# Keys and values laid out for their consumer: by strided matmul outputs and two sets of buffers, or by split VectorE writes and one set

## The reference, cut to what matters

```
xn = rms(x, g1)
Q = einsum('bsf,ef->bse', xn, Wq); K = einsum(..., Wk); V = einsum(..., Wv)   # 16 heads of 16
pQ = elu(Q); pK = elu(K)
Q1, Q2 = split(pQ, 2); K1, K2 = split(pK, 2)
kv1 = einsum('bshe,bshd->bsed', K1, V) * SCALE     # per token, over the heads
w1  = einsum('bshe,bsed->bshd', Q1, kv1)
attn = w1 - lmb * w2
```

## Time and profile before

| what | value |
|---|---|
| median of 3 runs | 1002.11 us |
| profiled execution | 997.24 us, its span 995.6 us |
| PE busy | 846.5 us (85%) |
| DVE busy | 644.6 us (65%) |
| ACT busy | 457.9 us (46%) |
| POOL busy | 258.8 us (26%) |
| DMA issues of K and V stores | 32 of 256 KB, median 3.5 us to landing |
| mean granted TensorE clock | 0.927 of full speed |

### The profile page before, as it was taken

The page is one execution under the profiler, slowest core; times in us unless marked ns, Lnnn a source line. Parts: engine busy times, 40 slices in busy tenths (PEclk is TensorE's granted clock), DMA queues, the critical chain, the costliest instruction groups (busy, mean ns, idle before and its releaser), DMA issues. The chain is left out here.

```text
span 995.6 us, 23453 instructions
## 1 busy us (share of the span) xinstructions
PE 846.5 (85%) x8964; PEld 700.0 (70%) x8964; DVE 644.6 (65%) x1464; ACT 457.9 (46%) x943; POOL 258.8 (26%) x323
## 2 busy tenths in 40 slices
PE   6999999998599999957999889988789649999940
PEld 5877778786377777735777778875567539999940
DVE  2577778777347777764555336678797876656438
ACT  2443443443477777735964324553533304444410
POOL 1146653122101123220000000022242043565323
PEclk9999999999699999987999989999989759999985
DMA  8400000000000000001476344452122213465437
GB/s 308 155 17 21 16 21 16 20 7 2 1 2 1 1 2 1 1 1 47 125 194 185 95 111 117 115 187 67 49 85 85 85 32 104 127 179 153 112 96 255
DMA packets 76428, 79.55 MB, mean 80 GB/s; under 512 B 22592, under 2 KB 66496, under 8 KB 75968
## 3 DMA queue, kind: packets, MB, share of 16 engines
q1 hardware_dynamic: 71376, 72.36, 23.5%
q0 software_dynamic: 3968, 5.25, 3.3%
q10 hardware_dynamic: 1008, 0.91, 0.3%
HBM read 50.71 MB, written 27.79 MB: 79 GB/s over the span
## 5 line engine op out<-in xcount | busy, mean ns | idle before, releaser
L712 DVE TENSOR_TENSOR r_prob<-r_pS,const 128x512 f32<-128x512 f32 x128 | 79.4, 682 | 32.4 <-PE r_pS L535 32.4
L1052 DVE SCALAR_TENSOR_TENSOR f_gl<-f_g,small_first,f_gh 128x512 fp32r<-128x512 f32 x64 | 47.3, 747 | 41.1 <-ACT f_gh L990 38.8
L931 PE MATMUL f_pY<-wpjT,f_gh 128*128 128x256 f32 x256 | 65.1, 289 | 0.0
L932 PE MATMUL f_pY<-wpjT,f_gl 128*128 128x256 f32 x256 | 62.7, 279 | 0.0
L931 PEld LDWEIGHTS f_pY<-wpjT,f_gh 128*128 128x128 f32 x256 | 48.1, 188 | 15.3 <-issue 13.4
L2223 POOL DMA_INDIRECT sum_dram<-e_yo,y_id x24 | 39.5, 1647 | 69.6 <-ACT e_yo L2312 61.8
L984 ACT ACTIVATE f_g<-f_pH 128x512 f32<-128x512 f32 x64 | 38.0, 594 | 39.2 <-PE f_pH L920 38.4
L838 POOL TENSOR_SCALAR t_ey<-t_es 128x8 f32<-128x8 f32 x4 | 1.0, 256 | 211.4 <-ACT t_sqrow L1770 211.4
L920 PE MATMUL f_pH<-f_xh,wfcT 128*128 128x512 f32 x128 | 53.2, 415 | 1.4 <-DVE f_xl L1046 1.4
L2342 DVE SCALAR_TENSOR_TENSOR e_hl<-e_pH,e_hh 128x320 fp32r<-128x320 f32 x64 | 27.7, 484 | 38.5 <-ACT e_hh L2305 38.4
L920 PE MATMUL f_pH<-f_xl,wfcT 128*128 128x512 f32 x128 | 51.8, 405 | 0.0
(11 more groups left out here) (292 smaller groups left out, 2447.8 us busy)
## 6 DMA issues: line engine op xcount, KB each, us to landing
kv_dram<-att_res SPq DMA_DIRECT2D x32, 256.0 KB, 3.5
t_ring<-kv_dram SPq DMA_DIRECT2D x128, 64.0 KB, 2.3
wi<-L_ffn_wi SPq DMA_DIRECT2D x8, 1024.0 KB, 5.7
wo<-L_ffn_wo SPq DMA_DIRECT2D x8, 1024.0 KB, 8.7
x_res<-L_attn_x SPq DMA_DIRECT2D x8, 512.0 KB, 5.0
q_dram<-att_res SPq DMA_DIRECT2D x8, 512.0 KB, 3.1
t_q<-q_dram SPq DMA_DIRECT2D x64, 64.0 KB, 2.8
x_dram<-x_res SPq DMA_DIRECT2D x8, 512.0 KB, 3.0
```

Of the source, the lines that this page charges most:

```text
L712: dve.tensor_tensor(prob[t % 2][:, r, :, :], pS[r][:, :, :], dec[:, r, :, :], ALU.mult)\
L931: pe.matmul(out, gh[c % 4][:, cols], net.wpjT[:, c, :], start=(c == 0 and t % 2 == 0), stop=False, skip_group_check=True)
L932: mm = pe.matmul(out, gl[c % 4][:, cols], net.wpjT[:, c, :], start=False, stop=(c == NH - 1), skip_group_check=True)
L1052: dve.scalar_tensor_tensor(out=gl[c % 4][:, :], in0=g[c][:, :], scalar=net.lnw[:, c:c + 1], in1=gh[c % 4][:, :], op0=ALU.mult, op1=ALU.sub ...
```

## The change

The special matmuls go. All six items become plain items: two matmuls of 128 columns by 512 tokens. The layout is made when the results are written to SBUF instead. For each K or V item, VectorE issues two instructions of 64 partitions by 512 elements: rows 0 to 63 and rows 64 to 127 of the item, both to partitions 0 to 63 of `res`, each to every fourth word (a step of 16 bytes). K and V are then stored by one transfer of 512 KB each, from 64 partitions, with 8 KB in one run for each.

There is one set of `res` in place of two. VectorE waits, at the head of each part, for the store of this part in the batch just before. The last V item of the last batch is written by ScalarE, behind a wait for the store of the batch before, and SyncE waits for a semaphore of its own for it. The counts in the waits of the fourth phase are changed to suit.

```diff
-    res = [[spare[:, (3 * p + n) * KD * SEQ:...] for n in range(3)] for p in two]
+    part = lambda n: spare[:, n * RUN * SEQ:(n + 1) * RUN * SEQ].rearrange("p (t i) -> p t i", i=RUN)
+    res = [part(n) for n in range(3)]
+    res_q = res[0].rearrange("p t i -> p (t i)")[:, 0:KD * SEQ].rearrange("p (k t) -> p k t", k=KD)
...
 # SyncE
-                sp.wait_ge(item_ready.sem, item_ready.after(ITEMS * b + KD * (n + 1)))
+                last = b == BATCH - 1 and n == 2
+                sp.wait_ge(item_ready.sem, item_ready.after(ITEMS * b + KD * (n + 1) - last))
+                if last:
+                    sp.wait_ge(last_value.sem, last_value.after(1))
...
-                    for h in two:
-                        sp.dma_start(tokens[h], res[b % 2][n][h * ROWS4:(h + 1) * ROWS4, :, :]).then_inc(kept, 16)
+                    sp.dma_start(net.kv_dram[n - 1, :, b * SEQ * RUN:(b + 1) * SEQ * RUN], res[n][0:ROWS4, :, :].rearrange("p t i -> p (t i)"))\
+                        .then_inc(stored[n].sem, 16)
...
 # ScalarE, behind the last batch
+        act.wait_ge(v_made.sem, v_made.after(2 * BATCH))
+        act.wait_ge(stored[2].sem, stored[2].after(16 * (BATCH - 1)))
+        for half in two:
+            dst = res[2][0:ROWS4, :, 2 + half]
+            ins = nc.scalar.activation(dst, pV[1][half * ROWS4:(half + 1) * ROWS4, :], ACT.Copy)
+        ins.then_inc(last_value.sem, 1)
...
 # TensorE
-                if n < 2:
-                    for k in range(KD):
-                        mm = pe.matmul(out[:, :], net.wqkvT[:, k, n * P:(n + 1) * P], xT[p][:, k, :], ...)
-                else:
-                    mm = interleaved(out, n // KD, n % KD, p)
+                for k in range(KD):
+                    mm = pe.matmul(out[:, :], net.wqkvT[:, k, n * P:(n + 1) * P], xT[p][:, k, :], ...)
...
 # VectorE
-            for n in range(ITEMS):
+            for n in range(ITEMS - (not behind)):
                 if n % KD == 0:
-                    dve.wait_ge(stored[part][p].sem, stored[part][p].after(STORES[part] // 2 * (b - p)))
+                    dve.wait_ge(stored[n // KD].sem, stored[n // KD].after(16 * b))
...
-                elif part == 1:
-                    ins = dve.tensor_scalar(to, rl[n % 2][:, :], 1.0, None, ALU.subtract)
-                else:
-                    ins = dve.tensor_copy(to, pV[n - 4][:, :])
+                for half in two if n >= 2 else ():
+                    dst = res[n // KD][0:ROWS4, :, n % KD * 2 + half]
+                    rows = slice(half * ROWS4, (half + 1) * ROWS4)
+                    if n < 4:
+                        ins = dve.tensor_scalar(dst, rl[n % 2][rows, :], 1.0, None, ALU.subtract)
+                    else:
+                        ins = dve.tensor_copy(dst, pV[n - 4][rows, :])
```

More of the change, by code:

```diff
@@ L1149, in _ @@
         norm(BATCH - 1)
-STORES = (16, 32, 32)
 def attention_inputs(net, ctx):
@@ L1169, in attention_inputs @@
     net.q_in = [Signal(net, net.ctx, f"q_in{i}") for i in two]
-    net.stored = [[Signal(net, net.ctx, f"kept{n}{p}", STORES[n]) for p in two] for n in range(3)]
+    net.stored = [Signal(net, net.ctx, f"kept{n}", 16) for n in range(3)]
     net.signals = own
@@ L1180, in attention_inputs @@
     rl = [ph.sb(f"rl{i}", [P, SEQ]) for i in two]
-    res = [[spare[:, (3 * p + n) * KD * SEQ:(3 * p + n + 1) * KD * SEQ].rearrange("p (k t) -> p k t", k=KD) for n in range(3)] for p in two]
+    res = [part(n) for n in range(3)]
+    res_q = res[0].rearrange("p t i -> p (t i)")[:, 0:KD * SEQ].rearrange("p (k t) -> p k t", k=KD)
     pX = [ph.ps(f"pX{k}", [P, SEQ]) for k in range(KD)]
@@ L1271, in front @@
             mm.then_inc(turned.sem, 1)
-        def interleaved(out, part, j, p):
-            for i in range(RUN):
-                cols = slice(part * DIM + i * ROWS4, part * DIM + (i + 1) * ROWS4)
-                for k in range(KD):
[L1278 to L1282, removed]
         def body(b, p, before, behind):
@@ L1292, in body @@
                     out, made = pV[n - 4], v_made
-                if n < 2:
-                    for k in range(KD):
-                        mm = pe.matmul(out[:, :], net.wqkvT[:, k, n * P:(n + 1) * P], xT[p][:, k, :], start=(k == 0), stop=(k == KD - 1))
-                else:
-                    mm = interleaved(out, n // KD, n % KD, p)
+                for k in range(KD):
+                    mm = pe.matmul(out[:, :], net.wqkvT[:, k, n * P:(n + 1) * P], xT[p][:, k, :], start=(k == 0), stop=(k == KD - 1))
                 mm.then_inc(made.sem, 1)
@@ L1475, in _ @@
                 for n in range(3):
-                    for kept in net.stored[n]:
-                        sp.wait_ge(kept.sem, kept.after(STORES[n] * (m + 2) // 2))
+                    sp.wait_ge(net.stored[n].sem, net.stored[n].after(16 * (m + 2)))
             if m >= 2:
@@ L1887, in scale_heads @@
                 for n in range(3):
-                    for kept in net.stored[n]:
-                        dve.wait_ge(kept.sem, kept.after(STORES[n] * BATCH // 2))
+                    dve.wait_ge(net.stored[n].sem, net.stored[n].after(16 * BATCH))
             dve.wait_ge(w_made.sem, w_made.after(4 * u + r + 1))
```

14 lines of the change are left out of this document (5 added, 9 removed).

## The result

The changed kernel takes 1005.79 us, the median of 20 runs (1002.14 to 1011.44); the kernel before, run beside it on the same chip, takes 1000.93 us (994.14 to 1005.06, 20 runs). The ratio is **1.0053**, with a 95% interval from 1.0033 to 1.0074: slower by half a per cent, some 5 us, which is within 1%. The profiled execution of after took 1002.86 us, its span is 1001.2 us against 995.6.

The account below looks back on a forecast made before the run. ScalarE was taken to bound batches 1 to 3 and PE the later ones, with VectorE taking over from batch 4. The batch 4 pause and VectorE's 12.05 us batches gave +5.1 us on 1002.11, stated as 1007; range 999 to 1030.

Parts of the forecast that it names:

- the pause for the Q store: At batch 4, VectorE waits for batch 3's Q store with one buffer set, starting at 515.9 instead of 510.00.
- DVE's pace behind it: From batch 4 on, VectorE becomes the bound at 12.05 us per batch, above PE's 11.6.
- its own case: Pause at batch 4 plus VectorE as bound from there: +5.1 us, range 1003 to 1012; chance 0.37.
- rival A: Strided writes are dear and the whole phase goes at VectorE's pace; over 10 us slower, up to 1035; chance 0.40.
- TensorE's part: Plain matmuls save only switches between matmul kinds: 0.34 us per batch, from 11.94 to some 11.6.
- ScalarE's pace: In batches 1 to 3, ScalarE with its ring clearing was taken to set the pace, 12.86 us per batch.
- The longer pitch: Alternating upper and lower row halves on VectorE don't overlap: 0.735 us from start to start for K, 1.085 for V.
- that leaves at 512.50 as before: On the SyncE queue, batch 3's Q store leaves at 512.50, with the clearing and 24 loads ahead unchanged.
- it should hold: PE's granted clock stays up through 2 us of idle time before batch 5; otherwise PE loses 2 or 3 us.
- counts only in batches 4 to 7: TensorE's 0.34 us gain per batch matters only in these batches, since ScalarE leads in batches 1 to 3.
- B: Writes cost little, 0.43 and 0.69 us, and the pause at batch 4 is swallowed; about +0.7 us, 1002.8; chance 0.20.
- C: The change doesn't do what it says, through a hidden matmul cost or a looser SyncE queue; 990; chance 0.03.

Follow-up runs that it names:

- e5: Changed kernel with both halves of each K or V item read from rows 0 to 63; phase 106.00 us, 1002.56 us, ratio 1.0024.
- e4: Changed kernel with K and V halves written densely instead of to every fourth word; phase 104.47 us, 999.80 us, ratio 1.0013.
- e1: Changed kernel with two sets of result buffers again; phase 107.03 us, 1001.96 us, ratio 1.0026.
- e3: Changed kernel with the 40 loads spread, 8 behind each of batches 2 to 6; phase 107.02 us, 1002.47 us, ratio 1.0032.
- e9: Changed kernel with the last V item's two halves in reverse order; phase 108.94 us, one run, 1004.0 us.
- e2: Kernel before with one set of result buffers in place of two; phase 106.90 us, 1000.91 us, ratio 1.0020.
- e6: Kernel before with all items by plain matmuls, full writes and two sets kept; phase 101.97 us, 997.46 us, ratio 0.9992.
- e7: Kernel before with the 12 ring clears on GpSimd in place of ScalarE; phase 110.81 us, 1005.31 us, ratio 1.0053.
- e8: Kernel before with ring clears spread over batches 0 to 3 and their loads later; run twice: phase 104.25 and 104.32 us, ratio 0.9972 and 0.9996.

## Why the prediction was right

It held in sign, in size (1007 for 1005.8) and in its mechanism: the pause for the Q store, and DVE's pace behind it. Some of the size is luck. The prediction gave its own case 0.37 and rival A 0.40, and what decided between them, the price of the write, it had to take from rows of another phase. The K half was taken too high and the V half too low, the pause ended later than predicted and DVE's batches were shorter, and two wrong readings, of TensorE's part and of ScalarE's pace, fell where they cost nothing. VectorE's chain, predicted and measured, by the start of item 0:

| | predicted | after |
|---|---|---|
| batch 4, behind the pause | 515.9 | 517.10 |
| batch 5 | 528.1 | 529.31 |
| batch 6 | 540.2 | 541.26 |
| batch 7 | 551.2 | 552.13 |
| last copy ends | 560.0 | 560.73 |
| SyncE's last store issued | 560.6 | 561.21 |

**The writes.** K half: 0.70 taken, the middle of 0.61 and 0.79, 0.624 measured, so the lower reading (the extra on half the elements) was the near one. V half: 1.05 taken, 1.082 measured. The longer pitch was right, and e5 shows that it is the alternating rows that make it. A DVE batch was to take 12.05 us and takes 11.95. By e4 and e5 that is some 2.4 us of strided writing and 1.4 of held starts per batch. The price of the step by e4: 0.39 us for 512 strided elements is 0.77 ns each, the upper of the two figures that I had from L1863.

**The stores.** The wait on the Q store of batch 3 was the one that mattered, and e1 and e3 show it from two sides. Its size was off: DVE resumed 1.2 us later than predicted. The term that failed is "that leaves at 512.50 as before". The store left at 513.98, since the first 8 loads took 5.67 us to issue, and not 3.77. The prediction took the loads as unchanged and put the other stores at nothing, as SyncE is idle outside the load blocks. But the loads begin when the ring is cleared, and DVE's longer batches bring the last V store of batch 2 close ahead of them. In after it starts at 499.82, and the loads at 500.75. In before the queue had been still for 4.0 us when they began at 501.16; the stores of K and V ahead, in the timeline of SyncE of before:
```profile
493.94 3.21 SPq L1210 DMA_DIRECT2D kv_dram<-att_res  x4
```
The time between the end of the store's issue and the first load, and the issue of the 8 loads, behind a store of 512 KB:

| | e4 | e5 | e9 | e1 | after | e3 |
|---|---|---|---|---|---|---|
| time between, us | 3.0 | 1.6 | 0.9 | 0.9 | 0.5 | 0.1 |
| 8 loads, us | 4.08 | 4.16 | 4.87 | 4.65 | 5.67 | 6.06 |

Behind stores of 256 KB it is 3.77 at 4.0 us and more (before, e2, e6) and 4.51 to 4.55 at 0.25 us (e7 and both runs of e8). So the issue is slower the closer the loads follow a store, and slower behind the larger one. After, e4, e5 and e9 issue the same stores and loads and differ only in how long VectorE writes, so the size isn't all of it; the size alone was never changed, and why the issue takes longer stays open. But the dearer writes lengthen the pause by this path, beside DVE's own pace.

**TensorE's part** was mis-sized, 0.34 us a batch for 0.76, and nothing came of it in after: DVE sets the pace there, at 11.95 against 11.18. The prediction's "it should hold" on the clock failed too. It assumed 2 us of idle time; there were 3.69, and the clock fell to 0.50. The store's delay and PE's shorter batches are what lengthened the idle time. The clock cost PE 8.82 - 7.03 = 1.8 us, which lay under DVE's lag, as the prediction had it for that case: DVE goes into item 0 of batch 5, at 529.31, without a wait.

**ScalarE's pace in batches 1 to 3** was wrong of the kernel before and right of the changed one. I had read two Exp starts 12.86 us apart as the pace of the phase; they were the pace of ScalarE alone, and PE's starts, which I had not put beside them, were 11.94 apart (shown under e8). With plain matmuls PE's starts become 12.8 apart from batch 2 to batch 4 (e6, after), so the gain "counts only in batches 4 to 7", as the sum had it, but for 0.5 us.

**The rivals.** A was to decide from 0.86 us for K and 1.2 for V; the halves are at 0.62 and 1.08. The figure of the Trainium skill that spoke for it ("Vector Engine (DVE) Microarchitecture Reference", section 5.2: 2.50 ns per element where the output steps by 24 words, measured there on a two-source program) doesn't describe this write: with a step of 4 words a V half takes 1.082 / 512 = 2.1 ns per element and a K half 1.2. B was right that the pause could be swallowed, but only on a VectorE with room, which is e2 and not after. C has nothing for it.

How the 5.9 us of the phase come about, by the runs: plain matmuls -3.1 (e6 against before), the split writes on that +5.1 (e1 against e6), the one set on that +3.9 (after against e1). The parts don't simply add: the one set alone costs 1.8 on the kernel before. Each is a difference of two single traces, and the load issue alone moves a phase with the pause by 1 us or more. Of the writes' +5.1, 2.1 come between the starts of batches 4 and 7 on TensorE (35.71 us in e1, 33.62 in e6: DVE's pace for PE's), and 2.8 behind batch 7's start (16.09 us to the end in e1, 13.29 in e6), where TensorE is through and DVE still has its last writes to do.

## What to carry to other kernels

Price a wait by the slack of the engine that takes it: the same wait cost 1.8 us where VectorE had 4.5 us per batch to spare and 3.9 where it had none, and a change that spends slack and adds a wait pays for both. In an in-order queue look at what stands ahead of the store that frees a buffer; moving loads behind it gave as much as a second set of buffers. Longer work can also move a store closer to such a block of loads, and change the block itself. And before an engine's own interval is called the pace of a loop, put the starts of the engine that bounds it beside it.

## What the runs showed of the hardware

- A change between 64-column matmuls of 128 tokens and 128-column ones of 512, or the transposes, costs TensorE 0.18 to 0.20 us, if the whole difference is put down to the changes (11.94, 11.58 and 11.18 us per batch with four, two and no changes). An item by 64 small ones takes 3.64 to 3.65 us beside changes, and one by 8 big ones 3.63 beside them and 3.44 without (before, e6).
- One-source f32 writes on VectorE with a step of 16 bytes: +0.39 us per 512 elements out of PSUM (0.688 to 1.082), +0.20 out of SBUF (0.421 to 0.624) (e4, after).
- A VectorE instruction that reads from rows 64 on behind one that read the same memory from row 0, or the other way, starts behind the end of the last one, 0.17 to 0.20 us later than it otherwise does (e5). Reads of SBUF and of PSUM count apart (e9).
- TensorE's granted clock fell to 0.50 when it began again after 3.69 us of idle time (after) and 3.19 us (e9), and stayed at 1.00 after 2.38 (e4) and 2.41 us (e5).
- GpSimd memsets of 1.9 us each held VectorE's SBUF to SBUF `tensor_scalar` for about one memset each (0.35 to 1.8 or 1.9 us), and its `scalar_tensor_tensor`, also out of SBUF, not at all (0.67 to 0.69 us). No copy out of PSUM fell among them (e7).
- The issue of 8 loads of 64 KB took 3.77 us with the queue still for 4 us ahead of them, 4.5 close behind a store of 256 KB, and 4.1 to 6.1 us behind one of 512 KB, most where it stood closest. The cause stays open.
